# Four graph layers on one core: half of layer 1's points moved up into layer 0, the other half into layer 1, nine products moved to GpSimd

## The chip, the cores and the metric

One core of a Trainium2 chip runs the whole program. The metric is the device time of one execution in microseconds. The engines are TensorE (PE, matmuls into PSUM), VectorE (DVE), ScalarE (ACT), GpSimd (POOL) and SyncE (SP, which issues the loads); they run side by side and wait for each other through semaphores.

## What is computed

Four graph layers follow each other on x (4096 nodes, 64 channels) and adj (4096 x 4096, about 0.4% filled, with its diagonal). Each layer takes a layer norm and a relu of x and adds its result to x. Layer 0 is a plain aggregation, a linear map and a relu. Layer 1, cut to what matters:

```
def lorentz_linear(x, W, b, scale):
    h = x @ W.T + b
    time = sigmoid(h[:, :1]) * exp(scale) + 1.1
    xn = h[:, 1:]
    sq = clip(sum(xn * xn, axis=-1), 1e-08)
    s = (time * time - 1.0) / sq
    return concatenate([time, xn * sqrt(s)])
h = lorentz_linear(x, W, b, scale)
q = lorentz_linear(h, Wq, bq, scale_q)
k = lorentz_linear(h, Wk, bk, scale_k)
att = sigmoid((2.0 + 2.0 * (qm @ k.T)) / att_scale + att_bias)    # qm: q with its time negated
support = (adj * att) @ h
return support / sqrt(clip(abs(-inner), 1e-08))                   # inner: Lorentz norm of support
```

Layer 2 aggregates log maps on the Poincare ball (it needs adj's row sums, the degrees), and layer 3 a bounded number of neighbours with decay. Neither is touched.

## The kernel before

**Halves and tiles.** Nodes lie 128 to a partition in T = 32 groups; G = 2 halves of 16 groups (g = 0, 1) are the unit of node-wise work. A layer over adj runs two halves h of its result columns, and in each 32 tiles of 128 x 2048; s = 32 h + i counts the tiles. The order of work on each engine is written out by hand: each engine has its own block of instructions, and steps of other work are put behind a certain tile.

**Layer 0** (TensorE's `tile0`). For tile s VectorE makes the mask (`mask0`, line 1553, 128x2048) and adds the tile before last to the degree sum (`degree0`, line 1559). TensorE multiplies features by the tile (8 matmul records at line 577, f32) and counts neighbours before each one by two triangular products of the mask (bf16). ScalarE writes the counts as bytes (`make_code`, line 1118) and issues their store, for layer 3. There are four mask buffers: mask s waits for the counts of tile s - 3, so VectorE can be some two tiles ahead. In the second half the first half's result is finished beside the tiles: its bias map (`to_nodes`, TensorE behind tile 37), the update of x, and layer 1's layer norm (mean, `centre_l1`, `spread_l1`, `feats_l1`) on VectorE. The biases are cut in three bf16 parts by GpSimd (lines 494 to 505, from tile 1 on); the bias map waits for them.

**Between the layers.** Behind layer 0 come the second half's bias map, update and layer norm; the degrees (line 681: 32 matmuls with one column, and a filler `keep_at_work`, line 622, behind every second one); and all of the points. A point of tag h, q or k in half g is: `flip` (8 transposes, line 601) and a copy to SBUF by ScalarE (line 1071), `linear` (two bias rows, line 595, and 8 matmuls, line 611), squares and exp by ScalarE (lines 1146, 1147), `lorentz_sum` (line 1622) and `lorentz_ratio` (lines 1629 to 1650) on VectorE, log and exp by ScalarE for the root (`lorentz_roots`), `lorentz_factor` and `lorentz_point` (lines 1656 to 1673) on VectorE. q and k both map the flipped h point. q and k are then split in f16: ScalarE copies the high part, GpSimd (line 514) subtracts for the queries' low part, VectorE (`key_low`, line 1712) for the keys'. TensorE turns them with 32 (`fold`, line 712) or 16 (`fold_both`, line 732) transposes, and they are copied out of PSUM. h, q and k of half 0 and h of half 1 are complete before the first scores; so are the map, sum and ratio of q and k of half 1.

**Layer 1.** For tile s and column half u TensorE makes `scores` (8 matmul records, line 756), ScalarE the sigmoid (`sigm`, line 1193), VectorE the product with adj (`product`, line 1729, 128x1024), and one tile later TensorE gathers (`gather1`, 4 matmul records, line 577). `att` has two buffers, `prob` four, adj's ring four slots. TensorE's order in a tile is scores(s, 0), scores(s, 1), other steps, gather(s - 1, 0), gather(s - 1, 1). The last steps of q and k of half 1 stand behind tiles 1 to 14; the scaling of the last layer's weights (w3) behind tiles 16 to 20.

Of the kernel before, what the change touches and what calls it, by code (L numbers as in the profile page):

```python
# [13 lines left out]
F16 = mybir.dt.float16  # L14
# [8 lines left out]
N = 4096  # L23
D = 64
# [10 lines left out]
MADE = 8  # L35
CODES = 16
# [107 lines left out]
def graph_layers(nc, x, adj_t, codes, w0_t, b0, w1_t, b1, wq_t, bq, wk_t, bk, scalars, w2, b2, w3, b3, out):  # L144
    ctx = ExitStack()
    with ctx:
# [73 lines left out]
        HL = nodes(slot(5))  # L220
        HBk = [work[:, k * UNIT:(k + 1) * UNIT].rearrange("p (t c) -> p t c", t=TG) for k in (14, 6)]

        def HBq(g):
            return H[:, 0:TG, :] if g else nodes(slot(6))[:, 0:TG, :]
# [110 lines left out]
        POINTS = (("h", 0), ("h", 1), ("q", 0), ("k", 0), ("q", 1), ("k", 1))  # L335
# [18 lines left out]
        def _(sp):  # L354
# [48 lines left out]
            for s in range(RING, 2 * T):  # L403
                sp.wait_ge(sem("prob_ready"), 2 * (s - RING + 1))
                load(s % RING, tile(s))

            for n in range(NU):
# [6 lines left out]
                elif k < RING:  # L414
                    sp.wait_ge(sem("prob_ready"), 2 * (2 * T - RING + k + 1))
                else:
                    sp.wait_ge(sem("flipped"), G)
# [38 lines left out]
        def _(pool):  # L456
# [55 lines left out]
            for g in range(G):  # L512
# [59 lines left out]
        def _(pe):  # L572
# [25 lines left out]
            def flip(src, g, dst):  # L598

                for u in range(g * TG // 2, (g + 1) * TG // 2):  # L600
                    ins = nc.tensor.transpose(PS[:, dst * BANK + u * P:dst * BANK + (u + 1) * P],
                                              src[:, 2 * u:2 * u + 2, :], ident[:, :])
                return ins

            def linear(w, b, g, dst):

                for a in (2 * g, 2 * g + 1):
                    if b is not None:
                        bias_rows(b, dst + a)
                    for u in range(4 * a, 4 * a + 4):  # L610
                        ins = mm(PS[:, dst * BANK + u * P:dst * BANK + (u + 1) * P], TA[:, u * P:(u + 1) * P], w,
                                 start=b is None, stop=True, skip_group_check=True)
                return ins

            def copied_out(name, n=1):

                pe.wait_ge(sem(f"{name}_a"), n)
                pe.wait_ge(sem(f"{name}_v"), n)
# [37 lines left out]
            for h in range(2):  # L656
                if h:
                    pe.wait_ge(sem("codes_made"), 2 * T * h)
# [1562 lines left out]
```

## Time and profile before

| | us |
|---|---|
| three runs | 1047.86, 1051.47, 1052.21 |
| median | 1051.47 |
| profiled execution, its own time | 1044.31 |
| its span, first to last instruction | 1042.6 |
| PE busy | 980.6 (94%) |
| DVE busy | 850.0 (82%) |
| ACT busy | 750.8 (72%) |
| POOL busy | 298.0 (29%) |
| mean granted TensorE clock | 0.981 of full |

Busy time is of the whole span. Layer 0 lies at about 11 to 246 us, layer 1 at 293 to 533, and layers 2 and 3 behind them. In the profile PEld is the load of weights, which overlaps PE, and L577 is the line of a helper that several products go through. A time in brackets behind a timeline row is the idle time of its engine ahead of it, with what ended it. Long runs of the same operation are merged in one row with their count.

### The profile page before, as it was taken

What the parts mean: (1) busy time and instruction counts of PE and PEld (TensorE: products, weight loads), DVE (VectorE), ACT (ScalarE), POOL (GpSimd) and SP (SyncE); (2) the same over time, 40 slices, a digit from 0 to 9 for tenths busy, and PEclk for the clock granted to TensorE, in tenths of its full rate; (3) what the DMA queues carried; (4) which work ended last, traced back from release to release, by engine and by line L of the source; (5) the groups of instructions that cost most, each with busy time, mean ns of one, the idle gap of its engine ahead of it and who ended that gap; (6) DMA issues with size and microseconds to landing.
All of it is one profiled execution on the core that took longest, in us unless ns stands there. A gap on an engine that the chain in (4) does not pass through costs nothing.

```text
span 1042.6 us, 16458 instructions
## 1 busy us (share of the span) xinstructions
PE 980.6 (94%) x6171; PEld 475.1 (46%) x6171; DVE 850.0 (82%) x1080; ACT 750.8 (72%) x805; POOL 298.0 (29%) x140
## 2 busy tenths in 40 slices
PE   6999979999899999999989999999999999998888
PEld 2444444446644444435434444444455454333455
DVE  6999969998678676697769987878878978888883
ACT  4655545554477667686788989988888888997683
POOL 1069980000001000004015464434343444342001
PEclk9999989999989999999998999999999999999999
DMA  9989987994048899788753444555655553446662
GB/s 330 420 332 422 423 366 241 345 403 162 1 160 282 292 304 301 262 268 303 261 188 127 160 127 158 170 194 164 198 163 162 165 171 116 155 142 201 214 217 78
DMA packets 96350, 238.43 MB, mean 229 GB/s; under 512 B 16401, under 2 KB 45073, under 8 KB 79889
## 3 DMA queue, kind: packets, MB, share of 16 engines
q1 hardware_dynamic: 87056, 220.62, 61.5%
q10 hardware_dynamic: 9216, 16.78, 4.2%
q8 instruction: 49, 0.80, 0.3%
q14 instruction: 29, 0.23, 0.1%
HBM read 219.55 MB, written 17.83 MB: 228 GB/s over the span
## 4 chain that ended last, share of the span: by engine, by line
PE 62%; DVE 20%; ACT 9%; issue 7%; POOL 1%; DMA 1%; DVEq 0%; SPq 0%; ACTq 0%; POOLq 0%
PE PS L577 39%; PE PS L756 9%; DVE TB L1559 6%; PE PS L896 4%; PE PS L865 4%; DVE work L2078 2%; ACT work L1268 2%; ACT work L1276 2%; DVE work L2066 2%; DVE ring L2084 1%; ACT work L1279 1%; DVE work L2072 1%; PE PS L589 1%; DVE work L1729 1%; ACT work L1262 1%
## 5 line engine op out<-in xcount | busy, mean ns | idle before, releaser
L555 POOL TENSOR_TENSOR ring<-work,ring 128x1024 f32<-128x1024 f32 x57 | 135.3, 2374 | 232.8 <-DVE work L2078 232.7
L1729 DVE TENSOR_TENSOR work<-work,ring 128x1024 f32<-128x1024 f32 x128 | 152.9, 1234 | 58.0 <-ACT work L1193 57.9
L1193 ACT ACTIVATE work<-PS,att_sc 128x1024 f32<-128x1024 f32 x128 | 148.0, 1201 | 68.5 <-PE PS L756 59.5
L1118 ACT ACTIVATE work<-PS 128x1024 uint8<-128x1024 f32 x128 | 124.2, 1024 | 100.0 <-PE PS L577 99.9
L577 PE MATMUL PS<-ring,work 128*65 128x256 f32 (+1 forms) x600 | 190.4, 465 | 3.8 <-DVE work L2105 3.8
L577 PE MATMUL PS<-work 128*64 128x512 f32 (+2 forms) x800 | 151.5, 519 | 1.4 <-ACT work L1262 1.2
L2072 DVE SCALAR_TENSOR_TENSOR work<-PS,work 128x1024 f32<-128x1024 f32 x72 | 88.0, 1222 | 55.0 <-PE PS L577 46.5
L756 PE MATMUL PS<-work 128*64 128x512 f16 x1024 | 124.0, 384 | 3.0 <-ACT work L1193 1.6
L577 PEld LDWEIGHTS PS<-ring,work 128*65 128x65 f32 x600 | 80.6, 138 | 90.7 <-issue 65.5
L1268 ACT ACTIVATE work<-work 128x1024 f32<-128x1024 f32 x72 | 76.0, 1055 | 34.8 <-DVE work L2066 34.7
L756 PEld LDWEIGHTS PS<-work 128*64 128x64 f16 x1024 | 59.0, 111 | 79.4 <-issue 34.7
L577 PEld LDWEIGHTS PS<-work 128*64 128x64 f32 (+2 forms) x800 | 42.8, 120 | 106.8 <-issue 83.8
L2078 DVE SCALAR_TENSOR_TENSOR work<-work 128x1024 f32<-128x1024 f32 x72 | 87.8, 1220 | 2.7 <-ACT work L1283 2.2
L496 POOL CAST bcut<-bias 128x384 bf16<-128x384 f32 x1 | 86.6, 86634 | 0.1
L865 PE MATMUL PS<-TB,TA 64*128 64x512 f32 x288 | 81.3, 641 | 1.5 <-DVE work L2072 1.5
L1283 ACT ACTIVATE work<-work 128x1024 f32<-128x1024 f32 x72 | 75.9, 1054 | 9.3 <-DVE work L2072 6.8
L1276 ACT ACTIVATE work<-work 128x1024 f32<-128x1024 f32 x72 | 76.1, 1057 | 2.3
L577 PE MATMUL PS<-work,tri_above 128*64 128x512 bf16 x512 | 77.3, 382 | 0.0
L896 PE MATMUL PS<-ident,work 128*128 128x128 f32 x448 | 62.0, 282 | 14.7 <-DVE work L2078 13.8
L1279 ACT ACTIVATE work<-work 128x1024 f32<-128x1024 f32 x72 | 75.0, 1042 | 0.0
L577 PE MATMUL PS<-work,tri_rest 128*64 128x512 bf16 x496 | 74.6, 379 | 0.0
L1262 ACT ACTIVATE work<-PS 128x1024 f32<-128x1024 f32 x72 | 72.6, 1008 | 2.3 <-PE PS L577 2.2
(280 smaller groups left out, 1402.1 us busy)
## 6 DMA issues: line engine op xcount, KB each, us to landing
ring<-in_adj_t SPq DMA_DIRECT2D x96, 1024.0 KB, 5.4
ring<-in_adj_t SPq DMA_DIRECT2D x104, 512.0 KB, 4.1
work<-in_adj_t SPq DMA_DIRECT2D x32, 1024.0 KB, 8.6
codes<-work ACTq DMA_DIRECT2D x64, 256.0 KB, 7.2
ring<-codes SPq DMA_DIRECT2D x64, 256.0 KB, 4.6
H<-in_adj_t SPq DMA_DIRECT2D x24, 512.0 KB, 4.2
X<-in_x SPq DMA_DIRECT2D x2, 256.0 KB, 5.2
X<-in_x SPq DMA_DIRECT2D x1, 512.0 KB, 10.4
```

Of the source, the lines that this page charges most:

```text
L555: nc.gpsimd.tensor_tensor(near(n), sums(n), near(n), ALU.mult).then_inc(sem("near_ready"), 1)
L577: return mm(out_ap, lhsT, rhs, start=starts, stop=True, skip_group_check=True)
L756: ins = mm(o[half_rows(e), :], k_hl[:, jt * P + e * D:jt * P + (e + 1) * D], qs[:, i0:i0 + BANK], start=first, stop=not first)
L865: mm(z_banks(n)[:, q * BANK:(q + 1) * BANK], TA[half_rows(q), p * P:(p + 1) * P], TB[half_rows(q), S * STRIP:(S + 1) * STRIP], start=True, ...
L896: ins = nc.tensor.transpose(PS[:, c:c + P], sums(n)[:, q * BANK + i * P:q * BANK + (i + 1) * P], ident[:, :])
L1118: nc.scalar.activation(made[:, k, u:HALF:2], PS[:, (4 + 2 * u) * BANK:(6 + 2 * u) * BANK], ACT.Relu).then_inc(sem("codes_made"), 1)
L1193: nc.scalar.activation(att[:, u, :], PS[:, (4 + 2 * u) * BANK:(6 + 2 * u) * BANK], ACT.Sigmoid, bias=att_sc[:, 2:3], scale=att_sc[:, 1:2]) ...
L1268: nc.scalar.activation(lnr[:, n % ROT, :], root[:, n % ROT, :], ACT.Ln).then_inc(sem("lnr_ready"), 1)
L1276: nc.scalar.activation(sums(n), lnr[:, n % ROT, :], ACT.Exp, scale=0.5).then_inc(sem("root_ready"), 1)
L1729: V.tensor_tensor(prob[:, m % 4, :], att[:, u, :], ring[:, s % RING, u * UNIT:(u + 1) * UNIT], ALU.mult)\
L2072: V.scalar_tensor_tensor(sums(n), z_banks(n), 1.0, sums(n), ALU.max, ALU.add)\
L2078: V.scalar_tensor_tensor(sums(n), sums(n), TAU_MAX, lnr[:, n % ROT, :], ALU.min, ALU.mult)\
```

## The change

All of it is in the order of steps, the places of buffers and two methods. The second half of layer 0 is written out tile by tile on VectorE and ScalarE, and three `points0(i)` put h and q of half 0 wholly, and k of half 0 up to its map, squares and ratio, behind its tiles i. The root and point of k, and the turn of the keys, stay behind the layer. `points1(s)` puts all of half 1's points behind layer 1's tiles. There VectorE takes the inverse root itself (a bit trick and three Newton steps, 11 chained operations) and ScalarE takes the time's sigmoid in place of exp. In the tiles of POOLED GpSimd makes the second product. Sum and ratio are chained one by one. The degrees have no fillers between them; 12 stand around the turn of the keys. The diff, cut:

```diff
+POOLED = (2, 3, 4, 8, 9, 10, 17, 18, 19)
+def maker(m):
+    s, u = divmod(m, 2)
+    by_pool = sum(a <= s - (not u) for a in POOLED)
+    if u and s in POOLED:
+        return "prob_ready_p", by_pool
+    return "prob_ready", m + 1 - by_pool
 SyncE:
-                sp.wait_ge(sem("prob_ready"), 2 * (s - RING + 1))
+                for u in range(2):
+                    sp.wait_ge(sem(maker(2 * (s - RING) + u)[0]), maker(2 * (s - RING) + u)[1])
 GpSimd:
+            query_low(0)
+            for s in POOLED:
+                m = 2 * s + 1
+                pool.wait_ge(sem("att_ready"), m + 1)
+                pool.wait_ge(sem(f"adj_loaded{s % RING}"), LOADS0 + 16 * (s // RING + 1))
+                if m >= 4:
+                    pool.wait_ge(sem("agg1_done"), m - 3)
+                nc.gpsimd.tensor_tensor(prob[:, m % 4, :], att[:, 1, :], ring[:, s % RING, UNIT:2 * UNIT], ALU.mult)\
+                  .then_inc(sem("prob_ready_p"), 1)
+            query_low(1)
 (in aux_nodes)
+                if g == 0:
+                    pool.wait_ge(sem("agg1_done"), 2 * (T + TG))
 TensorE:
+            def points0(i):
+                if i == 5:
+                    (bias map of layer 0's first half, as before)
+                if i == 13:
+                    pe.wait_ge(sem("feats_ready_l1"), 1)
+                    flip(grp(cen, 0), 0)
+                if i == 14:
+                    pe.wait_ge(sem("flip_out"), 1)
+                    linear(wbd["l1"][:, :], 1, 0).then_inc(sem("lin_h"), 1)
+                if i == 18:
+                    pe.wait_ge(sem("feats1_ready"), 1)
+                    flip(HL[0], 0)
+                if i == 19:
+                    pe.wait_ge(sem("flip_out"), 2)
+                    linear(wbd["q"][:, :], 2, 0).then_inc(sem("lin_q"), 1)
+                if i == 25:
+                    fold_high(0)
+                if i == 27:
+                    fold_low(0)
+                if i == 29:
+                    pe.wait_ge(sem("qll_out_a"), 1)
+                    linear(wbd["k"][:, :], 3, 0).then_inc(sem("lin_k"), 1)
...
+            for t in range(T):
+                ins = mm(PS[:, 7 * BANK + t:7 * BANK + t + 1], TB[:, t * P:(t + 1) * P], ones[:, :], start=True, stop=True)
+            ins.then_inc(sem("deg_summed"), 1)
+            for _ in range(6):
+                keep_at_work(6)
             fold_both(0)
+            for _ in range(6):
+                keep_at_work(6)
+            pe.wait_ge(sem("feats_ready_l1"), 2)
+            flip(grp(H, 1), 1)
+            pe.wait_ge(sem("khl_out"), 1)
+            def points1(s):
+                (s == 1: linear h; 6: flip h's point; 7: linear k; 13: fold_both(1);
+                 16: linear q; 22: fold_high(1); 24: fold_low(1); 28: the sum of w3)
 ScalarE, behind make_code of tile i:
+                (i == 2: scales; 3: copy of the sums; 9: squares of the norm; 11: its root; 13: flipped_out;
+                 14: squares h; 16: root h; 18: flipped_out; 19: squares q; 21: root q; 23: high("q");
+                 25, 27: qhh_out, qll_out; 29: squares k)
+            lorentz_roots("k", 0)
+            high("k", HBk[0], grp(K2, 0), 0)
             (squares and root of the second half's norm)
+            folded_out("khl_out", k_hl0, 0, "khl_ready")
             nc.scalar.preload_act_table_set("sigmoid_and_others")
+            points1(s): (0: flipped_out; 1: squares h; 6: flipped_out; 7: squares k; 11: high k; 13: khl_out;
+                         16: squares q; 20: high q; 22: qhh_out)
 VectorE:
+            points0(i): (7: update0(0), tops; 8: sums_l1, centre_l1; 10: the four operations of att_sc; 11: spread_l1;
+                         13: feats_l1; 16: sum_and_ratio h; 18: feature_point; 21: sum_and_ratio q;
+                         23: query_point; 30: sum_and_ratio k)
+            for i in range(T):
+                mask0(T + i, i % RING0, ((T + i) // RING0 + 1) * 16, False)
+                degree0(int(i >= 2), T + i - 2, (i - 2) % RING0)
+                points0(i)
+            for s in (2 * T - 2, 2 * T - 1):
+                degree0(1, s, s % RING0)
+            copy_out("sums_out0_v", TA[:, UNIT:2 * UNIT], PS[:, UNIT:2 * UNIT], ("agg0_done", 2 * T))
+            key_point(0)
+            update0(1)
+            sums_l1(1)
+            centre_l1(1)
             key_low(0)
+            spread_l1(1)
+            (degrees out of PSUM)
+            feats_l1(1, H)
+            def inverse_root(tag):
+                ratio, y, v = (grp(k, 1) for k in TAGS[tag][2:5])
+                hold(0)
+                chained(0, V.tensor_scalar(y.bitcast(I32), ratio.bitcast(I32), -0.5, 1597463007.0, ALU.mult, ALU.add))
+                for _ in range(3):
+                    hold(0)
+                    chained(0, V.tensor_tensor(v, y, ratio, ALU.mult))
+                    hold(0)
+                    chained(0, V.scalar_tensor_tensor(v, v, -0.5, y, ALU.mult, ALU.mult))
+                    hold(0)
+                    chained(0, V.scalar_tensor_tensor(y, v, 1.5, y, ALU.add, ALU.mult))
+                hold(0)
+                chained(0, V.scalar_tensor_tensor(v, ratio, 2.0, y, ALU.mult, ALU.mult))
+            points1(s): (2: sum_and_ratio h; 3: inverse_root h; 4: point h; 8, 9, 10: the same of k; 12: key_low;
+                         17, 18, 19: the same of q; 24: qll_out_v; 26, 30: w3)
             for s in range(2 * T):
                 product(s, 0)
-                product(s, 1)
+                points1(s)
+                if s not in POOLED:
+                    product(s, 1)
```

Lines in round brackets sum up code of the diff in words.

## Rows read from the trace of the kernel before

**Rows 1.** Busy time by stretch: PE, PEld, DVE, ACT, POOL, then PEclk, DMA share, GB/s

```profile
145.60:152.03 6.43, 0.01 (x1) 0.04 (x2) 1.73 (x1) 1.08 (x2) 5.91 (x7) 0.87 1.02 421
...
152.03:160.28 8.25, 8.25 (x42) 5.49 (x44) 3.69 (x6) 0.65 (x1) 0.00 (x0) 0.68 0.11 47
...
246.46:292.90 46.44, 36.54 (x334) 32.46 (x332) 34.56 (x89) 22.36 (x39) 2.13 (x1) 0.94 0.02 7
...
300.42:379.64 79.22, 79.22 (x613) 35.70 (x611) 62.03 (x65) 54.57 (x47) 3.08 (x1) 1.00 0.87 294
```

**Rows 2.** Timeline of layer 0's end: start, length, engine, line, operation

```profile
237.43 1.22 DVE L1553 TENSOR_SCALAR work<-work 128x2048 bf16<-128x2048 f32 x1
...
238.56 2.28 DVE L1559 TENSOR_TENSOR TB<-TB,work 128x2048 f32<-128x2048 f32 x1
...
239.48 1.88 PE L577 MATMUL PS<-work,H 128*64 128x512 f32 x8
...
240.77 1.22 DVE L1553 TENSOR_SCALAR work<-work 128x2048 bf16<-128x2048 f32 x1
...
242.92 1.88 PE L577 MATMUL PS<-work,H 128*64 128x512 f32 x8
...
245.07 0.60 PE L577 MATMUL PS<-work,tri_above 128*64 128x512 bf16 x4
```

**Rows 3.** Timeline of layer 0 around GpSimd's cast and the first bias map

```profile
61.06 86.63 POOL L496 CAST bcut<-bias 128x384 bf16<-128x384 f32 x1
...
145.05 2.28 DVE L1559 TENSOR_TENSOR TB<-TB,work 128x2048 f32<-128x2048 f32 x1
...
147.78 0.91 POOL L498 TENSOR_TENSOR brem<-bias,bcut 128x384 f32<-128x384 f32 x1
...
152.03 0.58 PE L595 MATMUL PS<-brow,bones 96*128 96x512 bf16 x1 [6.46 <-issue]
```

**Rows 4.** Timeline between the layers: maps, reduction, copy of a point, fold

```profile
266.72 0.38 PE L595 MATMUL PS<-brow,bones 96*128 96x512 bf16 x1 [0.33 <-ACT TA L1071]
...
268.94 0.38 PE L595 MATMUL PS<-brow,bones 96*128 96x512 bf16 x1
...
270.18 1.20 DVE L1622 TENSOR_REDUCE st<-work 128x16 f32<-128x1008 f32 x1 [4.82 <-ACT work L1146]
...
275.61 0.18 DVE L1671 COPY work<-time_h 128x16 f32<-128x16 f32 x1
...
284.79 1.08 PE L712 MATMUL PS<-identh,work 128*64 128x128 f16 x32 [2.12 <-ACT work L1071]
```

**Rows 5.** Timeline between the layers: first and last degree matmuls, table load

```profile
254.48 0.28 PE L681 MATMUL PS<-ones,TB 128*128 128x1 f32 x2
...
263.48 0.28 PE L681 MATMUL PS<-ones,TB 128*128 128x1 f32 x2
...
292.16 1.28 ACT L1184 ACT_TABLE_LOAD   x1
```

**Rows 6.** Timelines of GpSimd and VectorE in layers 1 and 2

```profile
326.81 3.08 POOL L514 TENSOR_TENSOR H<-H 128x1024 f16<-128x1024 f32 x1 [39.80 <-ACT H L1071]
...
328.08 4.01 DVE L1729 TENSOR_TENSOR work<-work,ring 128x1024 f32<-128x1024 f32 x2 [0.20 <-ACT work L1193]
...
564.15 4.14 POOL L519 TENSOR_TENSOR X<-X,work 128x1024 f32<-128x1024 f32 x1
...
564.85 1.22 DVE L2078 SCALAR_TENSOR_TENSOR work<-work 128x1024 f32<-128x1024 f32 x1
```

**Rows 7.** Timeline of layer 1, steady: VectorE, TensorE, ScalarE

```profile
385.18 2.36 DVE L1729 TENSOR_TENSOR work<-work,ring 128x1024 f32<-128x1024 f32 x2 [1.08 <-ACT work L1193]
...
386.31 1.90 PE L756 MATMUL PS<-work 128*64 128x512 f16 x16
...
387.39 2.30 ACT L1193 ACTIVATE work<-PS,att_sc 128x1024 f32<-128x1024 f32 x2 [1.14 <-PE PS L756]
```

**Rows 8.** Costliest groups: layer 2's products by GpSimd; busy and mean ns

```profile
L555 POOL TENSOR_TENSOR ring<-work,ring 128x1024 f32<-128x1024 f32 x57 | 135.3, 2374 | 232.8 <-DVE work L2078 232.7
```

More of the change, by code:

```diff
@@ L510, in _, with query_low @@
                 bias_piece(n)
-            for g in range(G):
+            def query_low(g):
                 pool.wait_ge(sem("q_high"), g + 1)
@@ L596, in bias_rows, with flip, linear @@
                           brow[0:96, b:b + 1, :].broadcast_to([96, BANK // D, D]), start=True, stop=True)
[L598 to L602, printed above, removed]
-                return ins
[L605 to L618, printed above, removed]
+            def flip(rows, g):
+                for n in range(TG // 2):
+                    u = g * TG // 2 + n
+                    ins = nc.tensor.transpose(PS[:, u * P:(u + 1) * P], rows[:, 2 * n:2 * n + 2, :], ident[:, :])
+                ins.then_inc(sem("flipped"), 1)
+            def linear(w, b, g):
+                for a in (2 * g, 2 * g + 1):
+                    bias_rows(b, a)
+                    for u in range(4 * a, 4 * a + 4):
+                        ins = mm(PS[:, u * P:(u + 1) * P], TA[:, u * P:(u + 1) * P], w,
+                                 start=False, stop=True, skip_group_check=True)
+                return ins
             def keep_at_work(bank):
@@ L670, in _ @@
-            pe.wait_ge(sem("feats_ready_l1"), 1)
-            flip(cen, 0, 0).then_inc(sem("flipped"), 1)
-            pe.wait_ge(sem("sums_out0_v"), 1)
-            to_nodes(wbd["l0"][:, :], UNIT, 2, 0).then_inc(sem("z0_ready"), 1)
-            pe.wait_ge(sem("codes_made"), 4 * T)
-            pe.wait_ge(sem("flip_out"), 1)
-            linear(wbd["l1"][:, :], 1, 0, 4).then_inc(sem("lin_h"), 1)
-            pe.wait_ge(sem("deg_added"), 2 * T)
-            def degrees(bank, spare):
-                for t in range(T):
-                    ins = mm(PS[:, bank * BANK + t:bank * BANK + t + 1], TB[:, t * P:(t + 1) * P], ones[:, :], start=True, stop=True)
-                    if t % 2 == 0:
-                        keep_at_work(spare)
-                ins.then_inc(sem("deg_summed"), 1)
@@ L686, in _ @@
-            degrees(7, 6)
-            for _ in range(4):
-                keep_at_work(6)
-            pe.wait_ge(sem("feats_ready_l1"), 2)
-            flip(H, 1, 0).then_inc(sem("flipped"), 1)
-            pe.wait_ge(sem("feats1_ready"), 1)
-            flip(HL, 0, 0).then_inc(sem("flipped"), 1)
-            pe.wait_ge(sem("deg_out"), 1)
-            pe.wait_ge(sem("flip_out"), 2)
-            linear(wbd["l1"][:, :], 1, 1, 4).then_inc(sem("lin_h"), 1)
-            pe.wait_ge(sem("flip_out"), 3)
@@ new lines, in _ @@
+            for k in range(MADE):
+                make_code(0, k, k, k, None)
+                if k == 2:
+                    square_first(2)
+                if k == 5:
+                    root_first(2)
+            with act.Fori(1, T // MADE) as it:
+                for k in range(MADE):
+                    make_code(0, it * MADE + k, k, it * MADE + k, it * 16)
+            for i in range(T):
+                make_code(1, T + i, i % MADE, i, (T + i) // MADE * 16)
+                points0(i)
```

460 lines of the change are left out of this document (229 added, 231 removed).

## The prediction, made before the changed kernel ran

> **What bounds the kernel now.** I first read busy time by stretch [rows 1], then the timeline of layer 0 (called the first layer here), of the passage behind it, and of layer 1 (the second), and last what GpSimd does beside VectorE. In the second half of the first layer TensorE starts a tile every 3.44 us (239.48, 242.92) and VectorE every 3.34 (237.43, 240.77), as 1.13 for the mask and 2.21 for the degree sum [rows 2]. Both are full. The last mask ends at 241.99 and is read at 245.07: VectorE is 3.1 us ahead. In the second layer TensorE is busy 79.22 of 79.22 us [rows 1] and needs 3.44 us a tile, ScalarE 2.30 and VectorE 2.36 [rows 7]; each of these two has 1.1 us to spare. Between the layers, from 246.46 to 292.90, one chain of points runs alone: 46.4 us [rows 1].
>
> So the place to gain is the 46.4 us, but most of it is TensorE work that is moved, not removed, and both layers that receive it are full on TensorE. Its prices [rows 4]: a linear map 2.2 us (bias row to bias row, 266.72 to 268.94), a flip, eight matmuls of it without a bias row, 0.9, a fold of 32 transposes 1.0. The first layer receives two flips, three maps and two folds: 1.8 + 6.6 + 2.0 = 10.4 us. The second receives three maps and one flip: 7.5; its folds were there before. What stays between is the bias map of the second half 2.2, the degrees 32 x 0.18 = 5.8 (from 254.48 to 263.48, less 16 fillers of 0.2) [rows 5], one fold and one flip: 9.8. Of 46.4 us only 46.4 - 10.4 - 7.5 - 9.8 = 18.7 were waiting and fillers. That is all that the change can win.
>
> **First layer, second half.** VectorE receives the sum and ratio of h, q and k (2.4 each: a reduction of 1.20 and seven small operations at about 0.2), the factor and point of h and q (2.2 each, up to the small copy at 275.61) [rows 4] and four small ones for the attention scale (0.9): 12.5 us. It was 3.1 ahead at the end; TensorE receives 10.4; so it would end 1.0 ahead and does not yet bind. Going tile by tile with these prices I find TensorE waiting twice, 0.6 us for the layer norm's features (now at tile 13 of the half) and 0.9 for h's point (tile 18): 1.5. So far the end of the layer moves by 10.4 + 1.5 = 11.9 us.
>
> **The low part of the queries is what I expect to decide.** GpSimd has to subtract it (line 514) between ScalarE's copy (tile 23 of the half, about 230 us) and TensorE's fold at tile 27. Until now this operation ran between the layers. The trace has a GpSimd operation that reads SBUF in this layer: the cast at 61.06 took 86.63 us. It ended at 147.69, 0.36 us after VectorE's last operation before a pause (145.05 + 2.28), and a larger one then took 0.91 [rows 3]. VectorE's mask and degree sum follow each other without a gap [rows 2]; GpSimd got no turn among some 26 tiles of them. Behind tile 23 VectorE again has nothing but these two until tile 30, where it waits for the squares of k, which need TensorE. By my tile count TensorE reaches the low fold at 241.4, VectorE goes on, with masks for two tiles more allowed, and stops at 251.0; GpSimd then takes 2.1 us (the 2.13 of rows 1) and TensorE goes on at 253.1: a stall of 11.7 us. After such a stall of 6.4 us (145.60 to 152.03) the granted clock was 0.68, and map and tile took 8.25 us in place of 2.2 + 3.44 [rows 1, 3]: 2.6 more. Together 14.3. Bounds: nothing, if GpSimd slips in; 14.3 if it has to wait, which is nearest to the only row. I take 14.3. The layer ends 26.2 us later.
>
> **Between the layers.** Mask 63 now comes behind the ratio of k, then three degree sums and the copy of the sums: 5.7 us from TensorE's last count. Then the bias map (7.9), degrees (13.7), fillers, fold and fillers (17.3), flip: scores start 18.2 us behind the last count if the clock holds. VectorE's chain beside it (key point 2.1, update 1.2, mean and centring 2.5, low keys 1.2, spread 1.4, features 2.2, with 0.5 of ScalarE) ends at 16.6 and hides under it; ScalarE's key copy and the table load of 1.28 [rows 5] end 1.0 behind the start. Waiting 5.7 us has its nearest row in the 6.4 us that cost the clock, so 1.8 more: 20.0. The passage shrinks by 26.4. Ends: 28.2 and 24.
>
> **Second layer.** The start to tile 2 takes about 8.4 us in place of 7.5, since h's map (2.2) lies in the wait for the first product: +0.9. The flip and two maps behind it add 5.3.
>
> Then the products by GpSimd. One takes 2.37 us [rows 8], against 1.18 on VectorE. They do not run beside VectorE's own: two products that met the query subtraction took 4.01 in place of 2.36 [rows 6, 7], and a GpSimd addition took 4.14 because of VectorE's operation at 564.85, which has two inputs in SBUF [rows 6]. So in a pooled tile the two engines take turns. In three successive tiles these turns are 3 x (2.37 + 1.18) = 10.7, ratio chain 1.0 (the reduction lies beside GpSimd), root chain 11 x 0.21 = 2.3: 14.0 against 10.3 on TensorE. Turns that start when the first product is ready leave the last GpSimd product 3.6 us late for its gather, after the 1.3 us that the old order had in hand. If GpSimd breaks into the root chain it is 4.5; if the small operations are not held up it is 1.2, from sharing the products alone. The trace has no small VectorE operation with two SBUF inputs inside a long GpSimd one. I take 3.6, by the nearest row, a large one of the same form. Three groups (h, k, q): +10.9, ends 3.6 and 13.5.
>
> The Trainium skill, "SBUF — State Buffer", section "SBUF: two separate sides", says that the shared port pair is an exclusive lock held for a whole instruction, also by a VectorE operation with two SBUF inputs. By that rule the small chain operations are blocked too, and a group costs the 3.6; without it, 1.2. For large operations the trace agrees [rows 6]; for small ones no row shows it. "GPSIMD Engine Reference", section "Engine selection", would leave two-input elementwise work to VectorE, as about twice slower on GpSimd: the trace agrees with 2.37 against 1.18, and this speaks against the pooled products.
>
> Loads cost nothing: four ring slots cover tiles that are late by under 4 us. The loads' waits on two counters, the second half's key copy moved to ScalarE (1.1 us to spare per tile), the wait of the auxiliary rows for tile 47 (needed at tile 56) and the moved w3 steps cost nothing for the same reason; without that cover the key copy is 1.9.
>
> **Sum:** 26.2 - 26.4 + 0.9 + 5.3 + 10.9 = +16.9 us on the profiled execution of 1044.31 (span 1042.6), which lies 7.2 under the median of the three runs, 1051.47. On the median: 1068.4, told as 1068.
>
> **The rivals.** (1) *GpSimd gets its turn in the first layer, and its products hold up no chain*: 11.9 - 26.4 + 0.9 + 5.3 + 3.6 = -4.7, and with the clock kept between the layers -6.5: 1045 to 1047. This is the one on the other side, and it hinges on the subtraction of line 514 at tile 23: it decides if that ends before tile 27, within some 11 us of its issue. For it: other VectorE stretches with dependent small operations leave gaps. Against: 86.63 us. (2) *Turn in the first layer, but blocked chains in the second*: +2.6, 1054. (3) *The stall comes, but small operations aren't blocked*: +9.6, 1061. (4) *VectorE becomes the bound of the first layer*: it is only 1.0 us ahead at the end; were each chained operation 0.1 dearer (some 30 of them) the layer would end 2 us later, 1070. This only widens the range.
>
> **How the numbers follow.** The forecast with (4) inside it 0.55 (1061 to 1076), (3) 0.15, (2) 0.13, (1) 0.17. About 0.5%, 5 us, is what a measurement of this kernel can tell from no change. Most of (1) with its clock kept is beyond it, the rest within: faster 0.13; with (2) and the lower edge of (3) same 0.20; slower 0.67. The range 1048 to 1076 leaves out the fast part of (1), and above it the case in which every chain is broken into and the clock costs again.
>
> **What would show it.** Line 514's first subtraction lasting 15 to 25 us; a pause of TensorE of about 12 us near 241, with a granted clock near 0.7 behind it; the last count near 273; first scores near 293, hardly moved; tiles 3 to 5, 9 to 11 and 18 to 20 of the second layer longer by 3 to 4 us in sum each; GpSimd products of 2.37 with VectorE operations behind them stretched. If line 514 takes about 2 us the forecast is wrong by 14; if the pooled tiles stay at 3.44, by 11; if the passage is not near 20 us, my chain between the layers is wrong.

## The result and the profile after

The changed kernel takes 1061.67 us (median of 19 runs, 1050.84 to 1065.29) against 1047.19 for the kernel before in the same series (19 runs, 1038.90 to 1052.62): a ratio of 1.013 with an interval of 1.0102 to 1.0158. It is slower by 14.5 us. The prediction was 16.9 us slower, told as 1068 us with a range of 1048 to 1076; it stood on a median of three runs, 1051.47, and the 4.3 us by which the 19 runs lie lower are part of its distance from 1061.67. The sign and nearly the size are right, but two of its steps were wrong in opposite directions, and that is what the rest is about.

The profiled execution took 1060.16 us with a span of 1058.3 (before: 1044.31 and 1042.6), so the two profiles differ by 15.7 us of span and may stand for the medians. Engine busy time of the page of the profile after:

```profile
PE 989.1 (93%) x6155; PEld 476.2 (45%) x6155; DVE 857.8 (81%) x1087; ACT 752.9 (71%) x800; POOL 320.6 (30%) x149
```

I read both traces at the same five marks: TensorE's last count of layer 0, the first scores of layer 1, the scores of its tile 2, the pooled groups, and the end of layer 1.

| stretch | before | after | difference | forecast |
|---|---|---|---|---|
| start to last count done | 246.46 | 259.72 | +13.3 | +26.2 |
| from there to the first scores | 46.44 | 27.93 | -18.5 | -26.4 |
| first scores to scores of tile 2 | 7.52 | 8.57 | +1.05 | +0.9 |
| flip and two maps in layer 1 | | 6.1 | +6.1 | +5.3 |
| three pooled groups | | 11.9 | +11.9 | +10.9 |
| sum | | | +13.9 | +16.9 |

The last row can be tested: layer 2's first matmul starts at 527.49 before and 541.39 after, 13.9 later. The other 1.8 us of the span lie in layers 2 and 3, which the change does not touch, and I have no cause for them.

**Layer 0's second half.** The timeline of the profile after around the low part of the queries, VectorE, GpSimd and TensorE (start, length, engine, line, operation, idle before it and its releaser):

```profile
227.97 2.29 DVE L1620 TENSOR_TENSOR TB<-TB,work 128x2048 f32<-128x2048 f32 x1
...
229.25 2.99 POOL L529 TENSOR_TENSOR work<-work 128x1024 f16<-128x1024 f32 x1 [78.16 <-ACT work L1105]
...
230.17 3.15 DVE L1614 TENSOR_SCALAR work<-ring 128x2048 bf16<-128x2048 f32 x1
...
233.38 0.62 PE L606 MATMUL PS<-work,tri_above 128*64 128x512 bf16 x4 [1.27 <-DVE work L1614]
...
234.70 1.06 PE L684 MATMUL PS<-identh,work 128*64 128x128 f16 x32
```

The subtraction (line 514 before, 529 now) is issued in the middle of a degree sum, waits until that ends near 230.2, and gets its turn before the next mask, which takes 3.15 us in place of 1.22. TensorE waits 1.27 us for that mask and does the low fold at 234.70. That is all. Its other two waits in this half behind the bias map are 0.50 us for the features and 0.35 for h's point, for 0.6 and 0.9 forecast. The forecast had 15 to 25 us for the subtraction and a pause of 11.7 behind it. The bias cut, by contrast, starved in this kernel as in the one before [rows 3]. GpSimd's timeline of the profile after:

```profile
59.52 87.34 POOL L511 CAST bcut<-bias 128x384 bf16<-128x384 f32 x1
146.95 0.91 POOL L513 TENSOR_TENSOR brem<-bias,bcut 128x384 f32<-128x384 f32 x1
```

**Between the layers.** Busy time by stretch, then the timeline of the passage:

```profile
259.72:287.65 27.93, 22.07 (x121) 18.64 (x119) 16.23 (x22) 7.04 (x10) 0.00 (x0) 0.63 0.03 10
```

```profile
264.38 1.22 DVE L1543 COPY TA<-PS 128x1024 f32<-128x1024 f32 x1
...
265.66 0.61 PE L624 MATMUL PS<-brow,bones 96*128 96x512 bf16 x1 [5.86 <-DVE TA L1543]
...
269.57 10.87 PE L747 MATMUL PS<-ones,TB 128*128 128x1 f32 x64
...
280.30 2.72 PE L645 MATMUL PS<-tri_above,tri_rest 128*128 128x512 bf16 x6
280.47 0.19 DVE L1761 TENSOR_SCALAR deg<-PS 128x32 f32<-128x32 f32 x1 [4.21 <-PE PS L747]
...
286.68 1.04 PE L631 MATMUL PS<-ident,H 128*128 128x128 f32 x8
287.65 1.92 PE L802 MATMUL PS<-Y,TA 128*64 128x512 f16 x16
```

TensorE's wait before the bias map is 5.86 us, as forecast (5.7). What follows is all slower than forecast: the map takes 3.9 us (265.66 to 269.57) for 2.2, the degrees 10.9 for 5.8, six fillers 2.72 for some 1.3. The granted clock is 0.63 over this stretch; before, with a wait of only 2.47 us there, it was 1.00 from 246.46 to 277 and 0.94 over the 46.44 us [rows 1]. By parts it was 0.55 in the map, 1.00 in the first 2.4 us of the degrees (269.57 to 272.00), and 0.50 from 274 to 285. So the clock fell twice: in the wait, and again in the degrees, in which TensorE had no pause.

The length is that of one execution. The same passage stands unaltered in six of the kernels of the experiments below. In the seven profiles, with a wait of 5.85 or 5.86 us in each, it takes 26.5 to 30.5 us; in the three longest the clock is 0.50 in all of the degrees, and these take 13.65 us. VectorE's chain is not what ends last: it waits 4.21 us for the degrees.

**Layer 1.** Timeline of the profile after in the first pooled group:

```profile
299.67 2.37 POOL L539 TENSOR_TENSOR work<-work,ring 128x1024 f32<-128x1024 f32 x1 [67.43 <-ACT work L1238]
299.68 1.20 DVE L1646 TENSOR_REDUCE st<-work 128x16 f32<-128x1008 f32 x1
...
300.79 1.28 DVE L1656 SCALAR_TENSOR_TENSOR time_h<-time_h,esc,time_c 128x16 f32<-128x16 f32 x1
...
303.42 2.83 POOL L539 TENSOR_TENSOR work<-work,ring 128x1024 f32<-128x1024 f32 x1 [1.38 <-ACT work L1238]
303.94 2.33 DVE L1769 TENSOR_SCALAR st<-st 128x16 int32<-128x16 int32 x1
...
307.57 0.18 DVE L1772 TENSOR_TENSOR st<-st 128x16 f32<-128x16 f32 x1
307.62 2.35 POOL L539 TENSOR_TENSOR work<-work,ring 128x1024 f32<-128x1024 f32 x1 [1.38 <-ACT work L1238]
307.78 2.23 DVE L1774 SCALAR_TENSOR_TENSOR st<-st 128x16 f32<-128x16 f32 x1
...
310.36 1.23 DVE L1827 TENSOR_TENSOR work<-work,ring 128x1024 f32<-128x1024 f32 x1
...
311.64 1.94 PE L606 MATMUL PS<-work,TA 128*64 128x512 f32 x8 [2.53 <-DVE work L1827]
```

Operations on 128x16 that otherwise take 0.17 to 0.25 us last until GpSimd's product is done, and the third product comes in the middle of the root chain. The reduction, with one input, isn't held up: it takes 1.20 us beside the product, as before [rows 4]. The product of the last tile of the group is then late and TensorE waits 2.53 us. The scores of the five tiles concerned start at 296.22, 299.67, 303.11, 307.21 and 313.41: 17.19 us for four tiles in place of 13.78, 3.4 more. The second group is the same (323.95 to 341.13, 3.4); the third takes 17.90 (361.97 to 379.87, 4.1 more) and the tile behind it 1.0 more, at a granted clock of 0.76 (379.8 to 384). The gather at 377.39, behind TensorE's wait of 2.53 us, took 2.70 us there and 1.94 in the other two groups, so some 1.7 of the third group's 5.1 us is clock. Forecast were 3.6 each. The flip adds 1.2 us (313.41 to 318.03, less 3.44), each map 2.5 (318.03 to 323.95 and 356.05 to 361.97): 6.1.

### The profile page after: what moved, and what is told of

It is laid out like the page before. It is cut to its first block, busy times and chain, and to the rows that moved or that the text cites. A ratio compares the mean times of both kernels' runs of the same rounds, so it can differ in the third digit from the quotient of the medians.

```text
span 1058.3 us, 16415 instructions
## 1 busy us (share of the span) xinstructions
PE 989.1 (93%) x6155; PEld 476.2 (45%) x6155; DVE 857.8 (81%) x1087; ACT 752.9 (71%) x800; POOL 320.6 (30%) x149
## 4 chain that ended last, share of the span: by engine, by line
PE 63%; DVE 21%; ACT 9%; issue 6%; DMA 1%; SPq 0%; DVEq 0%; ACTq 0%
PE PS L606 41%; PE PS L802 7%; PE PS L930 4%; PE PS L899 4%; DVE TB L1620 4%; DVE work L1827 2%; ACT work L1329 2%; ACT work L1337 2%; DVE work L2154 2%; DVE work L2142 2%; DVE work L1614 1%; DVE ring L2160 1%; ACT work L1340 1%; ACT work L1238 1%; PE PS L618 1%
## 5 line engine op out<-in xcount | busy, mean ns | idle before, releaser
L1827 DVE TENSOR_TENSOR work<-work,ring 128x1024 f32<-128x1024 f32 x119 | 141.2, 1222 | 66.9 <-ACT work L1238 66.9
L606 PE MATMUL PS<-work 128*64 128x512 f32 (+2 forms) x544 | 91.1, 486 | 4.2 <-DVE work L1827 2.5
L511 POOL CAST bcut<-bias 128x384 bf16<-128x384 f32 x1 | 87.3, 87345 | 0.1
L930 PE MATMUL PS<-ident,work 128*128 128x128 f32 x448 | 62.0, 282 | 15.2 <-DVE work L2154 14.3
L1620 DVE TENSOR_TENSOR TB<-TB,work 128x2048 f32<-128x2048 f32 x32 | 73.1, 2284 | 0.1
L1620 DVE TENSOR_TENSOR TB<-TB,ring 128x2048 f32<-128x2048 f32 x30 | 68.5, 2284 | 0.0
L606 PE MATMUL PS<-work,TA 128*64 128x512 f32 x256 | 62.2, 598 | 6.1 <-DVE work L1827 5.1
```

The source lines that it names most:

```text
L606: return mm(out_ap, lhsT, rhs, start=starts, stop=True, skip_group_check=True)
L930: ins = nc.tensor.transpose(PS[:, c:c + P], sums(n)[:, q * BANK + i * P:q * BANK + (i + 1) * P], ident[:, :])
L1620: V.tensor_tensor(TB[:, h * HALF:(h + 1) * HALF], TB[:, h * HALF:(h + 1) * HALF], ring0(k), ALU.add)\
L1827: V.tensor_tensor(prob[:, m % 4, :], att[:, u, :], ring[:, s % RING, u * UNIT:(u + 1) * UNIT], ALU.mult)\
```

## The experiments

Three questions were open. Why is the cast starved and the subtraction, over the same VectorE work, not? What makes the passage 8 us longer than forecast? And is the loss in layer 1 the turns of the two engines, or who does the product? The runs went in three series, each beside its own runs of the kernel before (medians 1046.63, 1047.82 and 1047.14).

### First series: the form of the cast, the pooled products, the wait in the passage

**GpSimd's first cast in another form.** The five casts and copies of the bias became two-input additions of zeros, the kind of operation that the subtraction is:

```
-link(nc.gpsimd.tensor_copy(bcut[0][:, :, :], bias[:, :, :]))
+link(nc.gpsimd.tensor_tensor(bcut[0][:, :, :], bias[:, :, :], brow[:, :, :], ALU.add))
```

> The changed kernel with GpSimd's five casts and copies of the bias cut in layer 0 written as two-input additions (of a tile of zeros). Same values. Theory F (form decides): in the changed kernel the two-input subtraction of the queries got in between a degree sum and a mask after 1.0 us, so an operation of that form does, while a one-input cast does not; then the first cut takes 1 to 4 us in place of 87, the biases are there long before tile 37, TensorE's stall of 6.4 us and its clock loss of 2.6 are gone: 8 to 9 us faster than the changed kernel. Rival P (position decides, the subtraction met VectorE at a lucky moment): the addition takes over 80 us again and the time does not move.

1062.79 us, ratio 1.0142 (1.009 to 1.0195). GpSimd's timeline of this kernel:

```profile
60.71 87.41 POOL L511 TENSOR_TENSOR bcut<-bias,brow 128x384 bf16<-128x384 f32 x1
```

The form of the operation does not decide.

**No pooled products**, and **two in a group in place of three**:

```
-POOLED = (2, 3, 4, 8, 9, 10, 17, 18, 19)
+POOLED = ()                          # and in the other kernel (2, 4, 8, 10, 17, 19)
```

> The changed kernel with no product on GpSimd (POOLED empty). Theory T (the two engines take turns): in three tiles VectorE alone has 7.1 of products, 2.2 of sum and ratio, 2.3 of root chain, 1.4 of point, 13.0 in place of turns of 14.0 with their order of waits; four tiles from scores 2 to scores 6 take 15.0 to 15.5 us in place of 17.2 (steady: 13.8); in sum 5 to 8 us faster than the changed kernel. Rival C (the chained small operations themselves make the tile late and GpSimd relieves VectorE): the four tiles take 17.2 or more, and the time is the same or up to 6 us longer.

> The changed kernel with GpSimd's products only in the tile of sum and ratio and in that of the point, not in the tile of the root chain (6 of 9 products). Theory T: the root tile has 2.36 + 2.3 on VectorE with nothing to take turns with; group of four tiles 15 to 16 us, 3 to 6 us faster than the changed kernel in sum, near the kernel with none. Rival C: the root tile, now with both products on VectorE, is the worst: 17.2 or more, same or slower.

1055.34 us, 1.0077 (1.0054 to 1.01), and 1054.94, 1.0055 (1.0028 to 1.0082). Without them the four tiles take 15.82 us (scores at 295.27, 298.71, 302.98, 307.45, 311.09), with two of three 15.85 (298.48 to 314.33), with all 17.19. So the pooled products do not relieve VectorE: taking all nine away wins about 6 us over the changed kernel (1055.34 against 1061.67, in different series). Taking away only the three in the tiles of the root chains wins as much (1054.94): the other six cost nothing against none. But 15.8 is still 2.0 over 13.78: the other part of a group's loss is that the chains stand as a block in one tile, in which TensorE catches VectorE up.

**Fillers in the passage.** TensorE gets 14 filler matmuls in the wait before the second half's bias map:

```
+pe.wait_ge(sem("codes_made"), 4 * T)
+for _ in range(14):
+    keep_at_work(6)
 pe.wait_ge(sem("sums_out0_v"), 1)
...
-pe.wait_ge(sem("codes_made"), 4 * T)
```

> The changed kernel with 14 filler matmuls on TensorE between the last counts of layer 0 and the wait for the copied sums (some 3 us of the 5.9 us pause). Theory K (the pause lets the clock fall, and the slow clock is what doubles the degrees): the granted clock between the layers rises from 0.63 to above 0.9, the bias map takes 2.2 in place of 3.9, the 32 degree columns 5.8 in place of 10.9, the passage 20 to 22 us in place of 27.9: 6 to 8 us faster than the changed kernel. Rival D (the degrees are dear without fillers between them, by their weight loads, whatever the clock): the clock rises, the degrees still take 10 us or more, the passage shrinks by 2.

1058.65 us, 1.0104 (1.0062 to 1.0147). Its passage is 24.6 us (253.83 to 278.44), 3.3 shorter. Timeline of its passage on TensorE:

```profile
255.07 3.19 PE L645 MATMUL PS<-tri_above,tri_rest 128*128 128x512 bf16 x14 [1.17 <-ACT work L1154]
259.76 0.39 PE L624 MATMUL PS<-brow,bones 96*128 96x512 bf16 x1 [1.49 <-DVE TA L1545]
...
260.88 0.38 PE L624 MATMUL PS<-brow,bones 96*128 96x512 bf16 x1
...
261.99 9.37 PE L749 MATMUL PS<-ones,TB 128*128 128x1 f32 x64
271.22 2.72 PE L645 MATMUL PS<-tri_above,tri_rest 128*128 128x512 bf16 x6
```

The map is back at 2.2 us (259.76 to 261.99), so the wait had cost its clock. But the degrees, now starting at the full clock, still take 9.4 us, and behind them six fillers take 2.72 again. This is neither theory as it stood, since it is not their price at the full clock: up to about 266.8 the granted clock is 1.00 and 10 to 12 records fall in each us, which would be 5.8 us for all 64; from 267 on it is 0.50, and 6 or 7 do. The mean from 253.83 to 278.44 is 0.79. So, one profile against one, the wait made 3.3 of the 7.9 us, and the larger part is the clock that falls within the degrees, with nothing between them.

This kernel's profiled execution (1051.23, the shortest of its six runs) showed something else, in GpSimd's timeline:

```profile
61.30 1.37 POOL L511 CAST bcut<-bias 128x384 bf16<-128x384 f32 x1
62.76 2.84 POOL L513 TENSOR_TENSOR brem<-bias,bcut 128x384 f32<-128x384 f32 x1
```

The same cast, over the same VectorE work, got its turn at the next boundary, each later piece too. The edit lies 190 us behind. Whether the cast is starved can thus differ between executions.

### Second series: the moment of issue, and the fillers in full

One theory said that it matters in which VectorE operation GpSimd's instruction is issued: behind a mask it is passed over, behind a degree sum it gets in. In both kernels I tied the pieces of the bias cut to the ends of degree sums, so that the cast is issued 0.2 us into a mask:

```
-    pool.wait_ge(sem("agg0_done"), 2 * n + 1)
+    if n:
+        pool.wait_ge(sem("deg_added"), 17 + n)
```

> The kernel before, with GpSimd's casts of the bias cut released by the end of a degree sum (18th to 24th), so that each meets VectorE just after the start of a mask; nothing else. Theory P (the moment decides: five profiles have the cast waiting 86 to 87 us when it is issued 1.0 to 2.0 us into a degree sum, one has it through in 1.37 us when it is issued 0.25 us into a mask): every piece takes 1 to 4 us, the 6.4 us pause before tile 38 and its slow clock go, 7 to 9 us faster than before, as in the three fastest of its runs (1039 to 1040). Rival R (whatever the moment, chance decides): the cast still waits past 100 us in the profile and the time does not move.

> The changed kernel with the same placement of the casts. Theory P: 7 to 9 us faster than the changed kernel, ratio 1.004 to 1.006 to the kernel before. Rival R: 1.013 as the changed kernel.

1047.17 us, 0.9996 (0.9975 to 1.0017), and 1062.45, 1.0139 (1.0111 to 1.0167). GpSimd's timeline of the first:

```profile
81.10 65.91 POOL L496 CAST bcut<-bias 128x384 bf16<-128x384 f32 x1 [21.62 <-DVE TB L1560]
147.09 0.91 POOL L498 TENSOR_TENSOR brem<-bias,bcut 128x384 f32<-128x384 f32 x1
```

Issued 20 us later and at another point of the pair, the cast ends at the same 147.0, with VectorE's first pause; in the second kernel it took 65.91 too. And the subtraction, placed the other way round, 0.2 us into a degree sum:

```
+pool.wait_ge(sem("mask_ready"), T + 26)
 query_low(0)
```

> The changed kernel with the queries' subtraction on GpSimd held until mask 57 is done, so that it is issued 0.1 us into a degree sum, one tile later than now (about 234 us). The forecast's step, conditioned on the moment: it waits until VectorE pauses at tile 30 of the half, 15 us or more, TensorE stalls by about 10 us, and the kernel is 8 to 13 us slower than the changed one. Rival G (this subtraction always gets its turn at the next boundary, as in all six profiles): about 4 us from issue to end, time within 2 us of the changed kernel.

1061.15 us, 1.0117 (1.008 to 1.0154). Timeline of this kernel:

```profile
232.49 2.28 DVE L1621 TENSOR_TENSOR TB<-TB,work 128x2048 f32<-128x2048 f32 x1
232.71 4.06 POOL L529 TENSOR_TENSOR work<-work 128x1024 f16<-128x1024 f32 x1 [80.42 <-DVE work L1615]
234.69 3.16 DVE L1615 TENSOR_SCALAR work<-ring 128x2048 bf16<-128x2048 f32 x1
```

It again got its turn at the next boundary. The moment by itself does not decide either: 1.0 us into a degree sum the cast was starved and 1.3 us into one the subtraction was not, and 0.2 us into a mask the cast was starved here and not in the profile of 1051.23. The pause of 11.7 us could not be provoked.

**Fillers between the degrees too**: the 14 of above, one behind every second degree matmul, the fold moved among them, the 12 fillers behind them dropped, and VectorE's features ahead of its copy of the degrees:

```
     ins = mm(PS[:, 7 * BANK + t:7 * BANK + t + 1], ...)
+    if t % 2 == 0:
+        keep_at_work(6)
+    if t == 19:
+        fold_both(0)
...
```

> The changed kernel with 14 fillers before the copied sums, a filler behind every second degree matmul as in the kernel before, the keys turned in the middle of the degrees, the other 12 fillers left out, and the layer norm's features ahead of the degrees' copy on VectorE. Theory K2 (the degrees alone are too little work to hold the clock: with 14 fillers ahead they still took 9.2 us and it fell to half behind them): the granted clock stays near 1.0 and from last count to first scores it is 19 to 21 us in place of 27.9; 7 to 8 us faster than the changed kernel. Rival S (another chain, VectorE's or ScalarE's, takes over at once): 24 us or more, like the kernel with 14 fillers alone (24.6).

1052.82 us, 1.0051 (1.0023 to 1.008): 8 to 9 us below the changed kernel. Busy time by stretch of its passage, and TensorE's timeline in it:

```profile
260.88:279.96 19.08, 16.42 (x137) 13.85 (x138) 16.24 (x22) 7.14 (x10) 0.00 (x0) 1.00 0.04 15
```

```profile
268.96 0.28 PE L749 MATMUL PS<-ones,TB 128*128 128x1 f32 x2
269.10 0.38 PE L645 MATMUL PS<-tri_above,tri_rest 128*128 128x512 bf16 x1
269.32 0.50 PE L749 MATMUL PS<-ones,TB 128*128 128x1 f32 x4
...
278.96 1.07 PE L631 MATMUL PS<-ident,H 128*128 128x128 f32 x8
```

The granted clock is 1.00 all the way, and the passage is 19.1 us, against 27.9 in the changed kernel and 20.0 forecast. So the miss of the passage was TensorE's clock. But this is one execution. The two kernels at the end of the third series have the same passage, and in their profiles it takes 25.50 and 25.52 us, with the same waits of 1.17 and 1.49 us in it. TensorE's timeline of the first:

```profile
272.04 0.50 PE L749 MATMUL PS<-ones,TB 128*128 128x1 f32 x4
...
272.61 0.83 PE L749 MATMUL PS<-ones,TB 128*128 128x1 f32 x4
...
286.22 4.47 PE L803 MATMUL PS<-Y,TA 128*64 128x512 f16 x24
```

For its first 11.9 us the granted clock is 1.00 there too; then, with TensorE at work without a pause and a filler behind every second degree matmul, it is 0.50 to the flip (272.60 to 284.34). So these fillers don't always hold the clock, and what decides wasn't found. The edit also put the fold among the degrees, dropped 12 fillers and changed VectorE's order, and what these gave by themselves wasn't measured; nor were the fillers between the degrees without the 14 in the wait.

### Third series: the same operation elsewhere, a deliberate pause, and the best version

**The cast itself in the second half.** The same cast is issued once more, just before the subtraction (it rewrites the same values):

```
+pool.wait_ge(sem("q_high"), 1)
+link(nc.gpsimd.tensor_copy(bcut[0][:, :, :], bias[:, :, :]))
 query_low(0)
```

> The changed kernel with one more cast of the bias on GpSimd (128x384, as the one that waits 87 us in the first half), released by the queries' high part, ahead of the queries' subtraction (about 229 us). Theory O (it is the operation: this cast gets no turn, the subtraction does): the cast waits until VectorE pauses at tile 30 of the half, some 20 us, TensorE stalls before the low fold by 10 to 12 us and comes back at a low clock, 10 to 14 us slower than the changed kernel: the forecast's step in full. Theory S (it is the stretch: something of the first 147 us keeps GpSimd out, not of this one): the cast is through in 1.5 us, the subtraction after it in about 4, and the time is within 2 us of the changed kernel.

1057.71 us, 1.0097 (1.0064 to 1.0131). Timeline of this kernel:

```profile
60.51 87.19 POOL L511 CAST bcut<-bias 128x384 bf16<-128x384 f32 x1
...
229.99 1.37 POOL L533 CAST bcut<-bias 128x384 bf16<-128x384 f32 x1 [78.06 <-ACT work L1107]
230.91 1.53 DVE L1616 TENSOR_SCALAR work<-ring 128x2048 bf16<-128x2048 f32 x1
```

One operation, one kernel, one execution: 87.19 us at 60.5 and 1.37 at 230. It isn't the operation. The place in the program goes with it, but doesn't settle it either, since the cast got through at the first place once. The time is 4.0 us under the changed kernel's, more than the 2 us expected, from four runs in another series; the two intervals of the ratio overlap.

**A pause for GpSimd.** In the kernel before, VectorE waits ahead of the mask of tile 36 for the finished bias rows:

```
+if k == 4:
+    dve.wait_ge(sem("brow_ready"), 3)
 mask0(T + k, k, (T // RING0 + 1) * 16, False)
```

> The kernel before, with one wait added: VectorE waits ahead of the mask of tile 36 until GpSimd has cut the biases. Whatever keeps GpSimd out, it ends with VectorE's first pause, and the rest of the cut then takes 4.9 us. At that tile VectorE is 5.4 us ahead of TensorE. Expected: the cast ends near 134, TensorE's 6.4 us pause before tile 38 and the 2.6 us of low clock are gone, but VectorE's lead is used up and it ends the layer about 2.6 us late: 5 to 8 us faster than the kernel before, ratio 0.993 to 0.995. If the pause is merely moved (VectorE's lead was worth nothing), the ratio is 1.000.

1042.5 us, 0.9963 (0.9942 to 0.9983). GpSimd's and VectorE's timeline of this kernel:

```profile
59.71 73.84 POOL L496 CAST bcut<-bias 128x384 bf16<-128x384 f32 x1
...
136.19 1.61 POOL L505 COPY brow<-bcut 1x384 bf16<-1x384 bf16 x3
...
137.84 1.23 DVE L1553 TENSOR_SCALAR work<-work 128x2048 bf16<-128x2048 f32 x1 [4.64 <-POOL brow L505]
```

The cast ends at 133.55 with VectorE's pause; the 4.64 us of VectorE lie in its lead, TensorE's pause of 6.46 [rows 3] is gone, and the last count is done at 239.76, 6.7 us earlier. In this profiled execution (1047.21, one of the long ones of its kernel) TensorE then waited 3.89 us before the second bias map in place of 2.47, and the granted clock in the passage was 0.74 to 0.83 in place of 1.00; tile 2 began at 301.47, 1.05 later than before. So in this profile nothing of the gain was left at tile 2. The median is 4.6 us lower, a little less than the 5 to 8 expected; that most runs keep the clock there better is likely, but no profile shows it.

**The parts put together.** First the changed kernel with the fillers of above, no pooled products, and each root chain dealt over two tiles, a chain's other parts a tile or two later; then the same with the pause:

> The changed kernel with all products on VectorE, the fillers placed as in e8_fillers, and the second half's chains spread: each root chain over two tiles, sum and ratio of h and q in two tiles (e.g. h over tiles 2 to 6 in place of 2 to 4). Theory T: each tile then has at most 2.36 + 1.4 on VectorE against 3.44 and the 1.3 in hand, so the 2.0 us that each group still loses without GpSimd's products goes; added to the gains of e2 and e8 (6 and 8 us) this is 16 to 20 us faster than the changed kernel, ratio 0.995 to 0.998. If the losses are not VectorE's tile budget, 1.000.

> e11_spread with e10's wait of VectorE ahead of the mask of tile 36. VectorE is fuller here (12.5 us more in this half), so part of the 9 us comes back as masks that are late: 2 to 6 us faster than e11, ratio 0.990 to 0.995. If VectorE becomes the bound of layer 0 at once, 0 or slower than e11.

1047.16 us, 0.9979 (0.9955 to 1.0002), and 1039.4, 0.9929 (0.9906 to 0.9953). TensorE's timeline of the first of them, in the first group:

```profile
296.21 1.90 PE L803 MATMUL PS<-Y,TA 128*64 128x512 f16 x16
...
309.98 1.90 PE L803 MATMUL PS<-Y,TA 128*64 128x512 f16 x16
```

Four tiles take 13.77 us: h's chain, spread, costs nothing. k's, whose sum and ratio stayed in one tile, still costs 1.4 us (18.59 for five tiles from 324.07) and q's 0.4. The last kernel is 7.7 us faster than the kernel before of its series. It and the pause by itself are the two whose intervals lie under both kernels. What the pause gives there is less sure: the medians are 7.8 us apart, more than the 2 to 6 expected, but the two profiles only 3.9, at tile 2 (292.28 and 296.21) as at the end. Runs of one of these kernels lie up to 9.3 us apart, and the clock that falls among the degrees in one execution and not in another makes 6.4 us (25.5 against 19.1).

## Why the prediction was right, and where it was not

**The sign** came from steps that held: the reckoning that only 18.7 us of the passage were waiting and fillers and the rest moves with its price; the start to tile 2 (+1.05 for +0.9); TensorE's wait before the bias map (5.86 for 5.7); and the pooled groups. For those the choice between 1.2 and 3.6 us was open, since no row showed a small VectorE operation with two SBUF inputs inside a long GpSimd one. Layer 1's fence above shows it at 307.78, and at 303.94 even a one-input operation on 128x16 of int32 takes 2.33 us. The groups measured 3.4, 3.4 and 5.1. By the rule of the Trainium skill ("SBUF — State Buffer", section "SBUF: two separate sides") the lock is held for the whole instruction, against VectorE operations with two SBUF inputs or in a 2-port mode. The trace agrees: 2.23 us for one with two inputs, and 2.33 for one with a single input, of which no row tells its mode. Part of the 3.6, though, is not the turns: without any pooled product a group still loses 2.0. And GpSimd did break into every root chain, which the prediction had at 4.5. Nor does the prediction show how 14.0 against 10.3, less the 1.3 in hand, becomes 3.6 and not 2.4, so its closeness to 3.4 is in part luck.

**The step that failed** is the low part of the queries, 14.3 us (11.7 of pause and 2.6 of clock). I took the cast's 86.63 us as the price of any GpSimd operation beside gapless masks and degree sums. The subtraction took 2.99 and cost TensorE 1.27, with no loss of clock (1.00 from 229 to 236); the sum without the step, 11.9, is close to the measured 13.3. The range's lower bound had named this case (nothing, if GpSimd slips in), and rivals 1 and 2 rested on it. With the turn and blocked chains it was rival 2, at +2.6.

**The term that was mis-sized** is the passage, 20.0 for 27.9 (26.5 to 30.5 over the seven profiles). I had 1.8 us for the clock in it, 18.2 without. The clock cost 9.5: the map 1.7, the degrees 4.9, the fillers 1.2 + 0.9, the fold 0.7, the flip 0.1 (from start to start in the timeline of the passage above, against the prices of the prediction); the other 0.2 are the wait. The degrees were priced at 0.18 each from a stretch in which a filler stood between every two [rows 5]; the change took those fillers away as waiting, and the wait and the bare degrees together lost the clock. With the wait filled and fillers between the degrees the passage is 19.1 in one profile and 25.5 in two. A smaller term of that kind is the flip and the maps, 6.1 for 5.3.

The two errors, 12.9 too much in layer 0 and 7.9 too little in the passage, together with 1.9 too little in layer 1, leave the sum 3.1 too high. That they nearly cancelled is luck. The forecast was right by more than its reasons were: rival 2 with the clock lost, +2.6 + 7.9 + 1.9 + 1.4 = +13.8, is what happened.

**What stays open.** Why GpSimd is passed over by VectorE from 60 to 147 us and not at 230 us. The form of the operation, the moment of issue and the operation itself are excluded by runs as what decides alone. What differs in the two stretches and was not tried: the loads' and ScalarE's traffic beside it, and the small dependent operations of VectorE that come some us ahead of the subtraction (224.67 to 226.93 in the profile after) and nowhere ahead of the cast. Since one execution let the cast through and others, with the same code up to there, didn't, some of it may be chance. Whether the runs that lie 7 to 11 us under their kernel's median are those in which the cast gets its turn, as in the one profile that showed it, is not shown; the two kernels with the pause, in which the cast can't hold up the bias map, spread by 8.1 and 8.9 us as well. Open too is what holds the clock among the degrees in one execution and not in another.

## What to carry to other kernels

Work that is moved under a full engine is paid for at its full price; count first how much of a gap is really waiting. Fillers that keep TensorE's clock are part of the price of what stands between them: without them, and behind a wait of 5.86 us, 5.8 us of short matmuls became 10.9 and more. Take more than one profile before you count on the clock: with the fillers back it stayed in one profile and fell in two. A VectorE chain that lies beside a saturated TensorE is hidden if it is dealt out in pieces smaller than the slack of one tile, and handing a product in the tile of the chain to GpSimd makes it worse (15.8 us for the group without, 17.2 with), because a product stopped small operations of the chain for its whole length; products handed over in the tiles beside it cost nothing.

## What the hardware showed that was not expected

- A GpSimd cast that takes 0.50 us alone (a later piece of the same size) took 86.4 to 87.3 us when issued near 60 us, in eight profiles; issued at 81 it took 65.9, and with an early VectorE pause 73.6 and 73.8. In all of these it ended with VectorE's first pause. Once it took 1.37, and at 230 us in one of these same programs 1.37 too.
- A pause of VectorE of 4.64 us, added inside its lead, took 4.6 us off the median of a kernel in which VectorE is nearly full (0.9963). Added to the other parts it took 7.8 off the median (1047.16 to 1039.4) and 3.9 between the profiles.
- GpSimd gets in between dependent operations of VectorE that follow each other within some 0.03 us (307.57 and 307.78 above), and holds up even small operations for the rest of its length: 2.33 us for a one-input one on int32 (303.94), while a one-input reduction beside another product kept its 1.20 us (299.68).
- The granted clock can fall from 1.00 to 0.50 while TensorE has no pause: 3 to 5 us into one-column matmuls with nothing between them (changed kernel; kernel with the 14 fillers), and in two of three profiles 3.8 us into the same matmuls with a filler behind every second one. 64 records of them take 5.8 us at 1.00 (estimate from 11 records per us) and 13.65 at 0.50. A wait does not decide alone either: behind 2.47 us the bias map ran at 1.00 in the kernel before, and behind 2.27 us, in the profile of the kernel with its casts placed, at 0.50 (249.36 to 251.60).
